# Gram products of a delta-rule attention layer: ScalarE copies both halves out of PSUM, GpSimd lays the causal mask on the query half

## What is computed

```python
def step(S, inps):
    qi, ki, vi, bi = inps
    pred = jnp.einsum('bhkv,bhk->bhv', S, ki)
    S = S + bi[..., None, None] * ki[..., :, None] * (vi - pred)[..., None, :]
    o = jnp.einsum('bhkv,bhk->bhv', S, qi)
    return (S, o)
```

## Time and profile before

| what | value |
|---|---|
| device time, median of three executions | 720.32 us |
| device time of the profiled execution | 717.71 us |
| its span, first to last instruction | 715.9 us |
| TensorE matmul busy | 587.2 us, 82% of the span |
| VectorE busy | 448.5 us, 63% |
| ScalarE busy | 257.6 us, 36% |
| GpSimd busy | 96.9 us, 14% |
| mean granted TensorE clock | 0.870 |

### The profile page before, as it was taken

How to read it: one execution, slowest core, us unless ns; L and a number is a source line. 1 busy time by engine, 2 the same in 40 slices (tenths; PEclk the granted TensorE clock), 3 DMA queues, 4 the chain that set the end, 5 groups by cost and what they waited for, 6 DMA issues and landing times.

```text
span 715.9 us, 17173 instructions
## 1 busy us (share of the span) xinstructions
PE 587.2 (82%) x7376; PEld 395.0 (55%) x7376; DVE 448.5 (63%) x1125; ACT 257.6 (36%) x571; POOL 96.9 (14%) x140
## 2 busy tenths in 40 slices
PE   1687980877799999796699769968689999999994
PEld 1544650467698867656498647854444444444442
DVE  4956495888868444847846972874665555555552
ACT  1365530654340635353434244243322222222221
POOL 2454471410000102100100010210200000000000
PEclk9988995875569999898758889997879999999998
DMA  9995003000000000000000410000212634344321
GB/s 333 320 369 222 1 20 99 0 2 2 2 2 5 4 2 2 2 2 1 1 3 4 136 55 2 5 1 1 66 30 66 173 88 112 85 105 114 88 60 29
DMA packets 19084, 46.78 MB, mean 65 GB/s; under 512 B 3809, under 2 KB 8545, under 8 KB 18753
## 3 DMA queue, kind: packets, MB, share of 16 engines
q1 hardware_dynamic: 18368, 45.43, 20.8%
q10 hardware_dynamic: 640, 0.26, 0.2%
HBM read 43.32 MB, written 2.36 MB: 64 GB/s over the span
## 4 chain that ended last, share of the span: by engine, by line
PE 60%; DVE 25%; ACT 4%; POOL 4%; SPq 2%; issue 2%; DMA 2%; DVEq 0%; POOLq 0%
PE psum L760 8%; PE psum L755 8%; PE psum L765 8%; PE psum L596 4%; PE psum L718 3%; PE psum L692 3%; PE psum L721 3%; PE psum L562 3%; PE psum L727 2%; POOL rstd L963 2%; SPq L410 2%; DVE yr L1302 2%; PE psum L623 2%; PE psum L466 2%; PE psum L681 2%
## 5 line engine op out<-in xcount | busy, mean ns | idle before, releaser
L942 ACT ACTIVATE arena<-psum 128x512 f32<-128x512 f32 x68 | 40.6, 597 | 133.3 <-PE psum L755 125.5
L1380 DVE TENSOR_TENSOR arena<-psum,arena 128x512 f32<-128x512 f32 x64 | 44.2, 691 | 62.2 <-PE psum L760 60.4
L765 PE MATMUL psum<-arena,wed_sb 128*128 128x512 f32 x128 | 67.0, 606 | 0.0
L783 ACT ACTIVATE arena<-psum 128x512 f32<-128x512 f32 (+1 forms) x72 | 34.3, 501 | 66.4 <-PE psum L562 40.8
L1385 DVE TENSOR_TENSOR arena<-arena 128x512 f32<-128x512 f32 x64 | 44.3, 692 | 14.7 <-PE psum L765 14.6
L562 PE MATMUL psum<-arena 32*64 32x128 f32 x1024 | 42.3, 322 | 9.9 <-DVE XA L1295 5.2
L562 PEld LDWEIGHTS psum<-arena 32*64 32x64 f32 x1024 | 36.2, 162 | 14.8 <-DVE XA L1295 5.9
L962 POOL TENSOR_TENSOR ve<-ss,eps_rms 128x4 f32<-128x4 f32 x16 | 4.3, 270 | 287.6 <-ACT yr L834 201.5
L765 PEld LDWEIGHTS psum<-arena,wed_sb 128*128 128x128 f32 x128 | 24.9, 194 | 31.6 <-issue 24.2
L760 PE MATMUL psum<-yT,weu_sb 128*128 128x512 f32 x68 | 37.3, 632 | 3.9 <-DVE arena L1380 3.9
L755 PE MATMUL psum<-yT,weg_sb 128*128 128x512 f32 x68 | 36.9, 626 | 2.2 <-ACT yr L783 2.2
(11 more groups left out here) (284 smaller groups left out, 1221.2 us busy)
## 6 DMA issues: line engine op xcount, KB each, us to landing
arena<-shares SPq DMA_DIRECT2D x64, 256.0 KB, 4.0
arena<-in_ctx_t SPq DMA_DIRECT2D x16, 514.0 KB, 8.4
arena<-in_ctx_z SPq DMA_DIRECT2D x16, 512.0 KB, 9.4
XA<-in_x SPq DMA_DIRECT2D x1, 1024.0 KB, 4.9
zlast<-in_ctx_last SPq DMA_DIRECT2D x4, 256.0 KB, 16.6
X<-x_mid SPq DMA_DIRECT2D x2, 512.0 KB, 4.5
weg_sb<-in_we_gate SPq DMA_DIRECT2D x2, 512.0 KB, 6.4
weu_sb<-in_we_up SPq DMA_DIRECT2D x2, 512.0 KB, 7.2
```

Of the source, the lines that this page charges most:

```text
L765: pe.matmul(x3, wed_sb[:, (p - 1) % (NPAIR + 1), :], act_a[pr], start=(p == 0), stop=False, skip_group_check=True).then_inc(x_down[pr], 1)
L783: return act.activation(out_, in_, ACT.Copy, scale=scale)
L942: act.activation(act_g[pr], banks[4 * pr + 2 * (n % 2)], ACT.Silu).then_inc(x_silu[pr], 1)
L1380: dve.tensor_tensor(act_gu[pr], banks[4 * pr + 1], act_g[pr], ALU.mult).then_inc(x_gu[pr], 1)
```

## The change

ScalarE copies the query half too, unmasked, into `BD`. The signal `g_a` now comes after both copies, and TensorE's next quarter waits for it alone. GpSimd multiplies the quarter of `BD` by the mask in place, in SBUF; it does so in its own loop over `STEPS`. The step o waits for all four masks of its group. VectorE's part of the gram steps is gone. The 32 quarter-and-group pieces (two layers, four groups, four quarters) are all treated alike.

```diff
# TensorE
-                            pe.wait_ge(g_diag[u], pi * 4 + q)
+                            pe.wait_ge(g_a[u], pi * 4 + q)
...
                     elif kind == "o":
                         pe.wait_ge(s_u[u], pi * 3 + 3)
+                        pe.wait_ge(g_diag[u], pi * 4 + 4)
# ScalarE
-                        copy(quarter(GA[g], q), gram_part(bank, 0)).then_inc(g_a[u], 1)
+                        copy(quarter(GA[g], q), gram_part(bank, 0))
+                        copy(quarter(BD[g], q), gram_part(bank, 1)).then_inc(g_a[u], 1)
# GpSimd
+                    elif kind[:4] == "gram":
+                        q = int(kind[4])
+                        pool.wait_ge(g_a[u], (l * 2 + pr) * 4 + q + 1)
+                        pool.tensor_tensor(quarter(BD[g], q), quarter(BD[g], q),
+                                           bc(tril.unsqueeze(1).unsqueeze(1), [P, 4, 2, T]), ALU.mult).then_inc(g_diag[u], 1)
# VectorE
-                    elif kind[:4] == "gram":
-                        q = int(kind[4])
-                        dve.wait_ge(g_a[u], pi * 4 + q + 1)
-                        dve.tensor_tensor(quarter(BD[g], q), gram_part(bank, 1),
-                                          bc(tril.unsqueeze(1).unsqueeze(1), [P, 4, 2, T]), ALU.mult).then_inc(g_diag[u], 1)
```

## The result

The changed kernel took 739.26 us in the median of four executions (734.3, 750.62, 736.78, 741.74), beside 720.16 us before. The ratio, which leaves out the slow execution of 750.62 us (granted clock 0.830), is 1.0201 with a 95% interval of 1.0134 to 1.0269, which is 14.5 us on 720.16 (9.7 to 19.4). The forecast of 729.5 us is 1.0127 times the old median: right in direction, just under that interval. The median lies 3.3 us over the range's upper end; the ratio makes it 734.6 us, inside the stated range of 717 to 736, though 0.6 us over the 734.0 that the likeliest case gave before the widening. The profiled execution took 734.3 us, its span is 732.5 (before 715.9) and its granted TensorE clock 0.854 (before 0.870).

The account below looks back on a forecast made before the run. VectorE's chain was taken to bound layer 0, TensorE layer 1. Layer 0's -6.5 + 0.5 - 0.4 + 14.7 = +8.3 us and layer 1's +1.8 make +10.1, named as 729.5 us, range 717 to 736.

Parts of the forecast that it names:

- the likeliest case: Whole kernel: GpSimd masks stall VectorE as worked out, 0.88 to 1.27 us each, 724.9 to 734.0 us; chance 0.64.
- the widening: Whole kernel: the likeliest case's 724.9 to 734.0 us was stretched to a stated range of 717 to 736.
- The five pairs: VectorE's chain, layer 0: mask multiplications of gram1 to gram3 A, gram1 and gram2 B leave, 1.29 us each, -6.5 us.
- the slack in the wait for TensorE's gram3 B: End of layer 0's inverse: TensorE finishes later than VectorE, and this slack was entered as -0.4 us.
- The squares of sq B: ScalarE, layer 0: they stand behind gram0 A's extra copy, so they and VectorE's sums come later, +0.5 us.
- Stalls: Layer 0: fourteen GpSimd masks beside VectorE's rs, kq, ext A and inverse cost 1.05 us each, +14.7 us.
- the prediction's rule: VectorE beside GpSimd: instructions with two SBUF inputs lose 1.05 us per GpSimd instruction, one-input reductions lose nothing.
- Rival (a): Layer 0's rs and ext: only scalar_tensor_tensor is stalled, six times; sum +1.7, 719.4 to 722.0 us; chance 0.18.
- Rival (b): Ext A and inverse of layer 0: no stall, VectorE relieved; sum -2.5, 715.2 to 717.8 us; chance 0.12.
- +8.3: Layer 0 at lout A: sum of the removed pairs, ScalarE, slack and stall terms, bounds +5.9 to +11.4 us.
- Layer 1: Ends of gram3 A and gram3 B: extra ScalarE copies and last masks delay ext, +1.1 and +0.7, sum +1.8 us.
- rival c: TensorE before and behind lout A: denser gram steps bring 2.4 GHz back sooner, -7 us; chance 0.04.

Follow-up runs that it names:

- e2: Changed kernel with the mask back on VectorE at its old place, in SBUF, ScalarE copying both halves: ratio 0.9988, kq A to lout A 49.76 us.
- e5: The kernel before with the change in layer 0 alone, first measurement: ratio 1.0159, kq A to lout A 57.77 us.
- e9: The kernel before with the change in layer 0 alone, second measurement: ratio 1.0129, kq A to lout A 57.60 us.
- e10: The whole change measured a third time, kernel unaltered: ratio 1.0233, kq A to lout A 57.73 us.
- e6: Kernel before, but ScalarE alone copies layer 0's five on-chain quarters and VectorE masks them later, first measurement: ratio 0.9945, kq A to lout A 45.28 us.
- e8: Kernel before, but ScalarE alone copies layer 0's five on-chain quarters and VectorE masks them later, second measurement: ratio 0.9938, kq A to lout A 45.25 us.
- r2: The whole change measured a second time, kernel unaltered: ratio 1.0178, kq A to lout A 57.90 us.
- e1: Changed kernel without the GpSimd masks and without o's wait for them: ratio 0.9978, kq A to lout A 45.47 us.
- e3: Changed kernel with each GpSimd mask replaced by two GpSimd memsets: kq A to lout A 45.48 us, executions 717.8 to 731.1 us, no ratio.
- e4: Changed kernel with GpSimd's masks held back to step wt, after their own stream's inverse: ratio 1.0025, kq A to lout A 45.40 us.
- e7: Changed kernel with each GpSimd mask replaced by a one-input GpSimd multiplication by 1.0: ratio 1.0074, kq A to lout A 49.73 us.
- e11: The kernel before with the change in layer 1 alone: ratio 1.0023, gram0 A to lin A 30.59 us.

## Why the prediction was right, and where it was short

**Removed.** The five pairs were costed at 6.5 us and the slack in the wait for TensorE's gram3 B at 0.4, 6.9 together. The stages without masks give 1.20, 1.21, 1.18 (after's 3.87) and, in the inverse with its slack, 2.74: 6.3 in all. The size of a pair was a little high: 1.29 adds two durations that overlap, and start to start a pair takes 1.20.

**ScalarE.** The squares of sq B were to come 0.5 later: 0.5 in e2, e5, e9 and e10. In the first profile it was 1.19, with half clock just before: the 15 us before kq A were granted 0.79, in before and in e10 0.92. The other runs with such a stretch (0.76 to 0.79) lie 0.9 to 1.6 over before, also e6 and e8, where no copy ahead of these squares was doubled. So the sums of kq A to lout A of the first profile, r2, e1, e3, e4, e6, e7 and e8 hold 0.6 to 1.1 us that are the clock's.

**Stalls.** Fourteen were counted, six in rs and kq, two in ext A, six in the inverse. The rows have fourteen, in those places, all six of the first group in rs. Two of the six were right by luck: the masks of 157.58 and 158.81 fall on tensor_scalar with one input, which by the prediction's rule lose nothing. Table: 6.02 (9.47 less 3.45), 1.83 and 6.01, 13.86 in all, so 0.99 us each where 1.05 was taken and 0.88 to 1.27 allowed. Rival (a) falls: the stalled instructions of the inverse are tensor_tensor. Rival (b) falls as a forecast; as a statement on what the edits are worth without a stall (-3.8 in layer 0) e1 bears it out with -4.2. By the price of the Trainium skill's SBUF — State Buffer page (Who interferes with whom), the whole instruction, the estimate of the term was 17.8; the measured 13.86 decides.

**Layer 0 and 1.** +8.3 was forecast at lout A; five profiles of the stalled layer 0 show +8.63, +8.21, +8.08, +7.91 and +8.04, the first two with half clock before kq A. Layer 1 was +1.8; the two stages give +2.0 (first profile), +1.4 (r2) and, alone in e11, +1.4, with a ratio worth 1.7.

**The step that fell short** is the sum itself, which has no term for TensorE's clock: it was weighed only as a gain (rival c), at 0.04, and not as a loss. The stages make 10.7 us in the first profile and 9.6 in r2, and about 9.4 where no half clock falls into them (8.0 and 1.4). The three measurements of the whole change make 13 to 17 (1.0178 to 1.0233). That the ratio's 734.6 us lies in the stated range is owed to the widening of the likeliest case's own range, for which the prediction names rivals (a) and (b) and not the clock; that is luck.

In the three profiles most of the remainder stands at a lower granted clock: 2.4 us before kq A, which no gram step precedes (0.82 from the start to kq A, before 0.86), and 1.9 between o A and o B (0.97, before 1.00) in the first; 2.3 before kq A (0.85) and 6.1 behind lin B (0.91, before 0.94) in r2; 4.1 less layer 1's 0.9 in e10's gram stage (0.85, before 0.98). In before, too, an execution at 0.870 took 717.03 us and one at 0.855 726.89. Part is chance, as e5 and e9 show.

Perhaps not all of it. Gram0 A to lin A of layer 1 took 33.6 to 33.8 us at 0.85 to 0.86 in five of the seven profiles of kernels in which VectorE lays no mask in either layer (e1, e3, e4, e7 and e10, but not the first and r2). In the seven others it took 29.7 to 31.4. So this dip stands more often where the masks have left VectorE in both layers than in the other kernels. Why is not shown: no run forces the clock. The three ratios of the whole change lie over the sum of its parts (1.0129 and 1.0159, with 1.0023), but the intervals overlap.

## What to carry to other kernels

Before work goes to an idle GpSimd, look at what VectorE runs in those microseconds: beside instructions with both inputs in SBUF, each two-input GpSimd instruction costs VectorE about its own length less one short instruction, and beside instructions that read one input from PSUM, nothing (e4). Rather than to another engine, such work can go to a later place on the same one: VectorE's own wait for lin B took stream A's six masks for nothing. And a shift of some microseconds also shifts where TensorE's half clock falls, so a gain at one stage is believed only with the stages behind it in view.

## What the runs showed of the hardware that was not expected

A tensor_scalar of 128x128 f32, with one SBUF input, is stalled as well: 0.22 us alone, 1.21 beside a mask, 0.44 to 0.55 beside a memset. A one-input GpSimd instruction of 1.49 to 1.60 us holds VectorE's tensor_tensor of the inverse only 0.28 to 0.39 us, a two-input one of 1.27 for most of its length (1.00 us on average). A GpSimd mask that reads one input and still masks was not tried.
